# Masked attention scores kept in their PSUM banks, and other queue orders in the first slots, the last slot and the end

## What is computed

```
h   = relu(layernorm(x))
x1  = x + c,   c = relu(max over the features of (adj @ h) + b)    # one number per node
h   = relu(layernorm(x1))                      # the same h: c shifts a whole row
q, k, v = h @ Wq + bq, h @ Wk + bk, h @ Wv + bv                    # 8 heads of 64
s   = q k^T / 8 + (adj == 0 ? -1e9 : 0)
out = x1 + softmax(s) v
```

## Time and profile before

| | us |
|---|---|
| median of 3 runs | 1313.68 |
| lowest and highest | 1312.29, 1314.34 |
| the profiled execution, its own time | 1313.61 |
| its span, first to last instruction | 1311.8 |
| PE busy | 1289.5 (98% of the span) |
| DVE, POOL, ACT busy | 1058.9, 1033.5, 944.9 |
| granted TensorE clock, mean | 0.996 of 2.4 GHz |

### The profile page before, as it was taken

One profiled execution on the slowest core, in us unless ns is written; L12 is line 12 of the kernel. 1 busy time (PEld: TensorE's weight loads), 2 busy tenths in 40 slices (PEclk: granted clock), 3 DMA queues, 4 the chain that ended last, 5 costly groups with the idle time before them and its releaser, 6 DMA issues.

```text
span 1311.8 us, 31156 instructions
## 1 busy us (share of the span) xinstructions
PE 1289.5 (98%) x11334; PEld 678.2 (52%) x11334; DVE 1058.9 (81%) x2207; ACT 944.9 (72%) x1461; POOL 1033.5 (79%) x1168
## 2 busy tenths in 40 slices
PE   7999999999999999999999999999999999999996
PEld 5455555555555555555555555555555555555554
DVE  7788888788788788788888888888887887887786
ACT  6877777777777777777777777777777777777555
POOL 5987877877877887887788788778778778778674
PEclk9999999999999999999999999999999999999998
DMA  5465655665565666556556655655555765764434
GB/s 195 84 139 125 139 135 130 131 137 136 122 145 137 122 137 137 130 131 143 130 124 145 136 122 144 139 121 138 135 131 132 138 135 124 143 137 114 101 79 113
DMA packets 434057, 171.72 MB, mean 131 GB/s; under 512 B 399337, under 2 KB 399474, under 8 KB 433906
## 3 DMA queue, kind: packets, MB, share of 16 engines
q1 hardware_dynamic: 433888, 169.72, 56.9%
q10 hardware_dynamic: 18, 0.00, 0.0%
HBM read 37.03 MB, written 33.55 MB: 54 GB/s over the span
## 4 chain that ended last, share of the span: by engine, by line
PE 92%; DVE 3%; ACT 2%; POOL 1%; issue 1%; DMA 0%; POOLq 0%; SPq 0%; ACTq 0%; DVEq 0%
PE proj L914 48%; PE proj L932 24%; PE proj L975 7%; PE sc L950 7%; PE proj L897 6%; DVE shifted L636 1%; DVE masked L624 0%; ACT h L439 0%; DVE row_max L628 0%; POOL h L327 0%; POOL inv_std L308 0%; POOL qkT L343 0%; ACT h L440 0%; DVE v L613 0%; DMA x_in<-in_x 0%
## 5 line engine op out<-in xcount | busy, mean ns | idle before, releaser
L914 PE MATMUL proj<-hT,w 128*128 128x512 f16 x3060 | 702.1, 379 | 0.6 <-ACT qk L453 0.6
L914 PEld LDWEIGHTS proj<-hT,w 128*128 128x128 f16 x3060 | 294.2, 98 | 353.3 <-ACT qk L453 1.1
L343 POOL TENSOR_TENSOR qkT<-qk,qkT 128x512 f16<-128x512 f32 x256 | 317.5, 1240 | 61.7 <-ACT qk L453 61.5
L932 PE MATMUL proj<-w,hT 128*128 128x512 f16 x1536 | 352.5, 379 | 2.6 <-DVE v L613 2.6
L350 POOL TENSOR_TENSOR probs<-probs 128x1024 f16<-128x1024 f32 x127 | 270.8, 2133 | 17.0 <-ACT probs L471 16.8
L469 ACT ACTIVATE probs<-shifted 128x1024 f16<-128x1024 f32 x127 | 134.2, 1057 | 180.4 <-DVE shifted L636 180.3
L451 ACT ACTIVATE qkT<-proj,bqk_up 128x512 f16<-128x512 f32 x256 | 173.4, 677 | 101.2 <-PE proj L914 97.5
L932 PEld LDWEIGHTS proj<-w,hT 128*128 128x128 f16 x1536 | 141.5, 98 | 154.5 <-DVE v L613 2.9
L613 DVE SCALAR_TENSOR_TENSOR v<-proj,v 128x512 f16<-128x512 f32 x128 | 88.4, 691 | 163.9 <-ACT v L459 163.9
L636 DVE TENSOR_TENSOR shifted<-masked,row_max 128x1024 f32<-128x1024 f32 x127 | 208.4, 1641 | 2.3
L658 DVE SCALAR_TENSOR_TENSOR y<-proj,out_scale,x 128x64 f32<-128x64 f32 x976 | 198.6, 277 | 4.3
(11 more groups left out here) (94 smaller groups left out, 1052.5 us busy)
## 6 DMA issues: line engine op xcount, KB each, us to landing
x_in<-in_x SPq DMA_DIRECT2D x128, 256.0 KB, 3.0
out_x<-y SPq DMA_DIRECT2D x128, 256.0 KB, 2.4
probsT<-probs SPq DMA_TRANSPOSE x127, 3.7
hT<-h SPq DMA_TRANSPOSE x124, 3.1
w_raw<-in_L_gnn_Wq SPq DMA_DIRECT2D x4, 256.0 KB, 5.4
w_raw<-in_L_gnn_Wk SPq DMA_DIRECT2D x1, 1024.0 KB, 7.9
w_raw<-in_L_gnn_Wv SPq DMA_DIRECT2D x1, 1024.0 KB, 11.0
bv_rows<-in_L_gnn_bv SPq DMA_DIRECT2D x1, 256.0 KB, 11.2
```

Of the source, the lines that this page charges most:

```text
L343: pool.tensor_tensor(qk_place(k, u, 1), qk32[:, u % 2, :], qk_place(k, u, 0), ALU.subtract).then_inc(qk_rest_done, 1)
L914: last = nc.tensor.matmul(proj[:, QK_BANKS[u % 2], :], w16[:, j, s, c, col * P:(col + 1) * P], hT[:, k // GROUP % HT_GROUPS, t, c, :, :].r ...
L932: last = nc.tensor.matmul(v_bank(m), hT[:, m // GROUP % HT_GROUPS, s, c, k % GROUP, :], w16[:, 2, t, c, :], start=(c == 0 and i == 0), sto ...
```

## The change

The SBUF tile `masked` is gone. DVE writes the masked scores back into the banks that they came from, reads them there for the maximum and for the subtraction, and PE's next scores for these banks wait for the subtraction (`shifted_done`) where they waited for the mask (`masked_done`). The other edits move calls within the queues: w of k's head in two halves on ACT, `normalise(10)` and `v_head(0)` in slot 5, the second half of q's rest ahead of `turn_out(3)`, w of v's peak ahead of slot 2 on DVE, `adjacency(0, 1)` into the middle of the first chunk on PE; in slot 127 and after it `qk_rest`, `probs_rest` and `add_bv` on POOL, `v_head` ahead of `exps` on ACT, and the products of graphs 124, 126 and 127 on PE. One of the two last groups of `warm` products goes, the other has 10 products for 24. Graph 124's result lies in `o_low`, not in the score banks.

```diff
@@ constants and tiles
-WARM_PRODUCTS = (32, 40, 20, 24, 12)
+WARM_PRODUCTS = (32, 40, 20, 10)
-        masked = sb("masked", [P, H, P])
+        def masked(m):
+
+            return score_banks(m).rearrange("p t (h n) -> p (t h) n", n=P)
+
-            return o_late if m in (B - 4, B - 2) else o_last if m == B - 1 else o_low
+            return o_late if m == B - 2 else o_last if m == B - 1 else o_low
@@ gpsimd: slot and end
-                probs_rest(base, k - ATTN_BEHIND)
+                if k < B - 1:
+                    probs_rest(base, k - ATTN_BEHIND)
                 qk_rest(base, k, u + 1)
-                add_bv(base, k - BV_BEHIND if k < B - BV_BEHIND else 2 * k - B + 1)
+                if k < B - 1:
+                    add_bv(base, k - BV_BEHIND if k < B - BV_BEHIND else 2 * k - B + 1)
...
+            probs_rest(B, -6)
             probs_rest(B, -5)
+            add_bv(B, -1)
...
@@ scalar: w_head(j, batch, parts=range(KC)), early_slot, slot, end
                 if k == 0:
                     normalise(base, 4)
-                elif k > 1:
+                elif k == 1:
+                    w_head(1, 2, (2, 3))
+                    normalise(base, 5)
+                else:
                     normalise(base, k + NORM_AHEAD)
                 qk_out(base, k, u + 1)
                 if k == 0:
-                    w_head(1, 2)
-                if k < 2:
-                    normalise(base, k + NORM_AHEAD)
+                    w_head(1, 2, (0, 1))
+                elif k == 1:
+                    normalise(base, 6)
...
-                v_head(base, k - V_OUT_BEHIND)
+                if k != V_OUT_BEHIND:
+                    v_head(base, k - V_OUT_BEHIND)
                 c_of(base, k)
-                normalise(base, k + NORM_AHEAD)
+                if k != ATTN_BEHIND:
+                    normalise(base, k + NORM_AHEAD)
                 qk_out(base, k, u)
+                if k == ATTN_BEHIND:
+                    normalise(base, k + NORM_AHEAD)
                 exps(base, k - ATTN_BEHIND)
                 qk_out(base, k, u + 1)
+                if k == ATTN_BEHIND:
+                    v_head(base, 0)
                 if k == B - 1:
+                    v_head(B, -V_OUT_BEHIND)
                     exps(B, -5)
...
-                act.wait_ge(out_scale_done, m + 1 if m < B - 2 else B)
+                act.wait_ge(out_scale_done, m + 1)
...
@@ vector: softmax (the same in softmax_shift and last_softmax), start, slots, end
-                    nc.vector.scalar_tensor_tensor(masked[:, :, :], score_banks(m).rearrange("p t (h n) -> p (t h) n", n=P),
+                    nc.vector.scalar_tensor_tensor(masked(m), masked(m),
...
-                    nc.vector.tensor_reduce(row_max[:, :], masked[:, :, :], AX.X, ALU.max).then_inc(max_done, 1)
+                    nc.vector.tensor_reduce(row_max[:, :], masked(m), AX.X, ALU.max).then_inc(max_done, 1)
...
+                    dve.wait_ge(out_scale_done, count - 1)
...
             w_rest(0, 1, (0, 1))
+            w_rest(0, 1, (2, 3))
             turn_out(3)
-            w_rest(0, 1, (2, 3))
...
             for k in range(B):
+                if k == 2:
+                    moments(k + MOMENTS_AHEAD)
+                    w_peak_of(2, 4)
                 if 0 < k < ATTN_BEHIND:
                     adjacency_out(0, k + 1)
                 slot(0, k)
-                if k == 2:
-                    w_peak_of(2, 4)
...
@@ tensor: waits, first chunk, end
-                    wait(pe, masked_done, m - 1)
+                    wait(pe, shifted_done, m - 1)
...
-                    elif m == B - 4:
-                        pe.wait_ge(masked_done, B - 1)
                     elif m == B - 2:
-                        pe.wait_ge(y_scaled, 3)
+                        pe.wait_ge(shifted_done, B - 1)
                     else:
-                        pe.wait_ge(y_scaled, 1 if m == B - 5 else 2)
+                        pe.wait_ge(y_scaled, m - B + 6)
...
-            first_chunk(0, range(KC))
+            first_chunk(0, range(2))
             adjacency(0, 1)
+            first_chunk(0, range(2, KC))
             first_chunk(1, range(KC))
...
+            scores(B, -1)
             v_rows(B, -2)
-            scores(B, -1)
+            probs_times_v(B, -4)
             v_rows(B, -1)
-            probs_times_v(B, -4)
             probs_times_v(B, -3)
-            pe.wait_ge(v_evac, B - 1)
+            probs_times_v(B, -2)
             warm(3, proj[:, AV_BANK, 0:P])
             turn_last_probs(0)
+            turn_last_probs(1)
             last_probs_times_v(0)
-            pe.wait_ge(v_evac, B)
-            warm(4, proj[:, QK_BANKS[1], 0:P])
-            turn_last_probs(1)
-            probs_times_v(B, -2)
             last_probs_times_v(1)

```

52 lines of the change are left out of this document (30 added, 22 removed).

## The result

| | before | changed |
|---|---|---|
| median (12 runs each) | 1312.63 us | 1310.10 us |
| lowest and highest | 1312.05, 1314.34 | 1309.07, 1310.73 |
| the profiled execution, its span | 1313.61, 1311.8 | 1309.07, 1307.3 |

The ratio of the changed kernel to the one before is 0.9977, with a 95% interval of 0.9969 to 0.9984: 2.5 us faster, where the prediction said 6.5 and a time of 1307.1. The time lies inside the prediction's range of 1304.8 to 1310.5, 0.4 us from its upper end. The profiled execution of the changed kernel is the fastest of its twelve, that of before lies 1.0 us over its median, so the two traces differ by 4.5 us and the medians by 2.5.

A forecast was written before the change was run, and what follows sets the result against it. The prediction took PE, busy in 98% of the span, as the bound, with only head and tail to win: 1313.61 - 0.5 (head) - 6.0 (tail) = 1307.1 us. Range 1304.8 to 1310.5, the forecast's own 1305.3 to 1308.6.

The forecast's parts named there:

- writing into PSUM: DVE's writes: taken at 1.28 us, as now; rival at double gives +3.8 us in the tail, 1310.9, chance 0.09.
- the 122 slots unchanged: Slots between head and tail: 3.6 us to spare before PE's scores wait for the subtraction, so 0 us more.
- the stretched subtraction: Rival: DVE's subtraction stays stretched beside POOL, no gain in the head; time 1309.6 us, chance 0.12.
- The head: Start of the kernel, up to graph 0's product: 0.5 us sooner, bounds 0 to -1.0.
- (b): Head: splitting w_head frees a q bank sooner but delays normalise(5) and POOL; with the first chunk's edits gain 0, at most 0.3.
- Step (c): Head: v_head(0) in slot 5 removes PE's 0.78 us wait at 63.38; graph 0's product starts at about 66.3.
- The end: Tail from 1262 us on, added up: 6.0 us sooner, span ending at 1305.8 for 1311.8.
- Graph 126's product: Tail, PE: waits for exponentials, POOL's 2.13 us and a 3.7 us landing until 1296.15, and ends at 1297.65.
- The second turn: Tail: starts at 1298.85, behind out_scale_of(126) and last_rest(1) on DVE; 6.96 us from there to the span's end.
- The half clock: Tail: PE at the 1.2 GHz level for graph 126's product, 1.48 us against 0.91; 0.7 us less at 2.4 GHz.
- the rival in which both ends do better: Rival for head and tail: clock kept and graph 7's transposition no hindrance; 1304.9 us or less, chance 0.06.
- the first chunk: Head: PE's first chunk takes adjacency(0, 1) into its gap, q's rest comes sooner; PE about 0.9 us early at 20 us.

The follow-up runs named there:

- e2: The changed kernel with the SBUF tile masked back and all new queue orders kept: 1312.01 us, ratio 0.9993 to the kernel before.
- e1: The kernel before with only the masked scores kept in PSUM, all queue orders as before: 1309.12 us, ratio 0.9973 to the kernel before.
- e4: The changed kernel with all its edits of the first slots undone: 1309.04 us, ratio 0.9972 to the kernel before.
- e5: The changed kernel with w of k's head whole again instead of in halves: 1309.73 us, ratio 0.9977 to the kernel before.
- e11: The changed kernel run again unaltered, on a second chip: 1310.15 us, ratio 0.9978 to the kernel before.
- e7: The changed kernel with graph 122's probs_rest ahead of the second qk_rest of slot 127 again: 1309.44 us, ratio 0.9976 to the kernel before.
- e9: The changed kernel with graph 126's product behind both turns on PE and out_scale_of(126) behind the copies on DVE again: 1306.80 us, ratio 0.9952.

## Why the prediction came out as it did

**The number.** 1310.1 us lies in the range of 1304.8 to 1310.5, but outside the forecast's own, 1305.3 to 1308.6, and the gain was 2.5 us of the 6.5 forecast. The upper part of the range was there for rivals that the traces refute: the subtraction isn't stretched any more (priced at 1309.6), and writing into PSUM isn't dear (1310.9). That the range holds is luck.

**Direction and cause of the slots.** Right: faster, the 122 slots unchanged (1193.87 and 1193.98 us), the gain at the ends alone.

**The operations.** Right in each number: the subtraction 1.22 us at all times, the mask 1.284 for 1.276, writing into PSUM next to free. The last was bounded from nothing to double and taken at nothing. The reduction rose by 5 ns, and the subtraction's shortest fell from 1224 to 1215. The Trainium skill, "VectorE: DVE Perf Modes", section on the TRN2 errata, has 62 cycles more from PSUM than from SBUF, by the clock that it gives an estimated 65 ns for each of the two operations that moved. The trace doesn't agree.

**What the stretch was worth.** As a rival the prediction priced the stretched subtraction at 2.5 us on the changed kernel; e2 measured 1.9. The mechanism, a subtraction that stretches beside GpSimd with both large inputs in SBUF and not with one in PSUM, was right. But the working gave most of the 6 us to the orders, and that step was wrong: the memory alone brings 3.6 (e1), the orders on top of it -1.0. The rival's price counted only graphs 123 and 126, and there are stretched subtractions at 125 and 127 too.

**The head, -0.5 forecast.** The term was wrong in sign for the edits, though not for the memory. Between the common point and graph 0's product the change is 0.2 to 0.3 us slower than before, made of -0.9 (memory) and +1.2 (edits). The step that failed is (b), "Everything won so far is held back there", with a gain of 0. The working saw that normalise(5) starts 1.15 us later and that POOL then has no pause, and let it end at no loss, with rest(7) at 41.0. It ended at 41.36, and its transposition landed 3.4 us later for 3.0: the chunk at 44.73 for 44.05, of which 0.2 are drift between the executions. Nor did the delay stay there: POOL came to graph 0's probabilities 48.61 us after the common point, for 48.35 before and 47.39 in e4, where the sum had it 0.4 to 0.5 sooner than before. Step (c) gave the 0.78 us of the v wait to v_head(0); e4 has no such wait without that edit, and what moving normalise(10) behind a q output leaves is 0.3 us against before (e5, 53.95 for 54.27) where 0.9 were to be had (e4).

**The end, -6.0 forecast.** The profiled execution shows -5.1, e11 -4.3 (46.81 for 51.12). The way there was right to some hundredths: masks 124, 125 and 126 were forecast at 11.72, 16.92 and 23.72 us after the last slot's scores and came at 11.76, 16.97 and 23.76. Against the sum's 45.1 us (1305.8 - 1260.68) that is 0.9 and 1.7 too much, and three terms behind mask 126 hold it:

- Graph 126's product was forecast at 35.47 and began at 35.93 in both, 0.35 of it from the landing: 4.05 us for 3.7. In the seven executions with this order (changed, e2, e4 to e7, e11) the landing took 3.73 to 5.26 us, 4.5 in the mean, all on the path; the longest seen before, 4.6, was only named as a risk.
- The second turn was put 1.2 us after that product (1297.65 to 1298.85), by DVE's queue alone. On PE the `warm` products and the first turn stand between: in e11 the product ends at 1298.31, and the first turn's copy starts at 1300.27, so the second turn begins near 1300.2, 1.9 us after it. This path the sum left out.
- From the second turn to the end of the span the sum had 6.96 us; both traces have about 7.5. Of the 0.5 more, 0.3 to 0.4 lie behind the last store's issue (2.8 and 2.9 us for 2.53).

The half clock that the sum assumed for product 126 was met in five of the seven executions. In the profiled one of the result it wasn't, which gave back 0.6.

**What the sum didn't ask.** It took the new order of PE's last products as given and added it up. Putting product 126 ahead of the turns was the dearest part of the change, 3.35 us (e9), and the prediction had both durations, landing and turns, in its sum; it said that PE stands idle for 3 us and went on.

**The base.** For the absolute time nothing hangs on it: 1307.1 forecast against 1309.07 in the profiled execution is 1.1 from the head and 0.9 from the end. For the difference it matters: the profiled execution before was 1.0 us over the median of twelve, and three runs didn't show it.

**Small slips of the working.** 60.89 + 2.12 + 3.7 is 66.71, not 66.75. The price of the rival in which both ends do better, 1304.9, isn't worked out: 0.7 us for the clock and 0.9 for the first chunk off 1307.1 give 1305.5.
